# Attention and mixture-of-experts kernel: inputs relaid, projection biases folded into centred weights, norms of tiles 4 to 31 in one chain

## What is computed

```python
x = x + layernorm(attention(layernorm(x)))
x = x + layernorm(ffn(layernorm(x)))
# attention, 16 heads of 8 features
v, q, k = h @ Wv + bv, h @ Wq + bq, h @ Wk + bk
q, k = elu(q) + 1, elu(k) + 1
# causal running sums over the sequence: s += k (outer) v,  z += k
out = (q . s) / (q . z + 1e-6)
return out @ Wo + bo
# ffn: one shared expert, and the best of 16 experts, weighted by sigmoid(logit)
```

## Time and profile before

| | |
|---|---|
| runs | 351.32, 351.48, 351.48 us; median 351.48 |
| profiled execution | 353.47 us, its span 351.6 us |
| TensorE busy | 266.0 us (76%) |
| VectorE busy | 284.8 us (81%) |
| ScalarE busy | 188.8 us (54%) |
| GpSimd busy | 193.1 us (55%) |
| mean granted TensorE clock | 0.912 |
| DMA packets | 20,275, 28.60 MB |

### The profile page before, as it was taken

The page is one execution under the profiler, slowest core; times in us unless marked ns, Lnnn a source line. Parts: engine busy times, 40 slices in busy tenths (PEclk is TensorE's granted clock), DMA queues, the critical chain, the costliest instruction groups (busy, mean ns, idle before and its releaser), DMA issues.

```text
span 351.6 us, 6328 instructions
## 1 busy us (share of the span) xinstructions
PE 266.0 (76%) x1493; PEld 189.3 (54%) x1493; DVE 284.8 (81%) x1147; ACT 188.8 (54%) x572; POOL 193.1 (55%) x221
## 2 busy tenths in 40 slices
PE   0449899999999995838887988730999999999100
PEld 0215565565656552524555755520999988988000
DVE  3599999999999999996998786560279999999940
ACT  1723566565656652447666563301799888885000
POOL 5064677777677773300055556371006888888870
PEclk9998999999999999877999899965699999999855
DMA  4999960000000000000011111126960101110100
GB/s 112 334 427 348 352 203 0 2 3 0 2 0 2 2 0 0 1 3 0 0 63 61 62 62 61 62 76 196 358 207 15 34 30 36 39 36 32 31 2 0
DMA packets 20275, 28.60 MB, mean 81 GB/s; under 512 B 2285, under 2 KB 15476, under 8 KB 19856
## 3 DMA queue, kind: packets, MB, share of 16 engines
q1 hardware_dynamic: 16624, 21.57, 18.2%
q0 software_dynamic: 3040, 6.37, 5.3%
q10 hardware_dynamic: 576, 0.26, 0.3%
HBM read 15.57 MB, written 13.60 MB: 83 GB/s over the span
## 4 chain that ended last, share of the span: by engine, by line
PE 39%; DVE 21%; POOL 17%; issue 12%; DMA 5%; ACT 1%; another core or an unknown queue 1%; SPq 1%; POOLq 0%; ACTq 0%; DVEq 0%
PE banks L1019 13%; POOL out L484 10%; POOL rows L478 5%; PE banks L1042 5%; DMA rows<-in_x 4%; PE banks L1106 3%; PE banks L1140 2%; PE banks L1048 2%; DVE hT L824 2%; POOL sorted_rows L468 2%; PE banks L1007 2%; PE banks L1040 1%; PE banks L1065 1%; PE banks L1063 1%; DVE stats L859 1%
## 5 line engine op out<-in xcount | busy, mean ns | idle before, releaser
L443 POOL TENSOR_TENSOR kv<-qk,vv 128x1024 f32<-128x1024 f32 x32 | 62.5, 1952 | 2.5
L1019 PE MATMUL banks<-kv,upto 128*128 128x512 f32 x128 | 61.3, 602 | 0.8 <-POOL kv L443 0.8
L1140 PE MATMUL banks<-xsT,w_now 128*128 128x128 f32 x376 | 53.8, 288 | 0.4 <-issue 0.4
L484 POOL DMA_INDIRECT out<-rows,token_i x47 | 46.9, 998 | 9.6 <-issue 8.0
L437 POOL TENSOR_TENSOR qk<-ex,rl 128x256 f32<-128x256 f32 x32 | 23.3, 729 | 50.4 <-ACT ex L542 50.4
L1140 PEld LDWEIGHTS banks<-xsT,w_now 128*128 128x128 f32 x376 | 48.1, 200 | 1.2 <-issue 0.5
L468 POOL DMA_INDIRECT sorted_rows<-rows,slot_i x32 | 31.6, 986 | 30.2 <-DVE slot_i L814 22.2
L728 DVE TENSOR_TENSOR prod<-banks,qk 128x1024 f32<-128x1024 f32 x32 | 38.9, 1217 | 2.7 <-PE banks L1019 0.8
L750 DVE TENSOR_REDUCE num<-prod 128x128 f32<-128x1024 f32 x32 | 38.7, 1208 | 0.3 <-DVE den L745 0.3
L958 DVE TENSOR_TENSOR hT_e<-silu_e,banks 128x256 f32<-128x256 f32 x47 | 19.3, 412 | 19.6 <-ACT silu_e L619 14.9
L478 POOL TENSOR_TENSOR rows<-rows,yn 128x128 f32<-128x128 f32 x40 | 19.2, 481 | 28.4 <-DVE yn L950 26.6
(11 more groups left out here) (152 smaller groups left out, 660.6 us busy)
## 6 DMA issues: line engine op xcount, KB each, us to landing
sorted_rows<-rows SPq DMA_DIRECT2D x3, 1950.0 KB, 12.0
rows<-sorted_rows SPq DMA_DIRECT2D x11, 520.0 KB, 6.2
w_exp<-in_gate_up SPq DMA_DIRECT2D x4, 1024.0 KB, 9.2
w_exp_down<-in_down SPq DMA_DIRECT2D x8, 256.0 KB, 8.8
out<-rows,token_i POOLq DMA_INDIRECT x47
rows<-in_x SPq DMA_DIRECT2D x1, 512.0 KB, 8.9
sorted_rows<-rows,slot_i POOLq DMA_INDIRECT x32
rows<-sorted_rows SPq DMA_DIRECT2D x1, 390.0 KB, 5.4
```

The lines of the kernel that those rows point to most:

```text
L443: nc.gpsimd.tensor_tensor(kv[:, u, :].rearrange("p (h m d) -> p h m d", h=NH, m=HD), k, v, ALU.mult).then_inc(s_kv, 1)
L484: nc.gpsimd.indirect_dma_start(out=out_rows, out_offset=bass.IndirectOffsetOnAxis(ap=token_i[:, j - 1:j], axis=0), in_=rows[:, j - 1, 0:D] ...
L1019: ins = nc.tensor.matmul(ps_s[u % 2][:, cols], upto[:], kv[:, u, cols], start=True, stop=True)
L1140: ins = nc.tensor.matmul(ps_gue[u % 2][:, c * P:(c + 1) * P], w_now[:, u % 2, c * P:(c + 1) * P], xsT[:, u % 2, :], start=True, stop=True)
```

## The change

x is given as [128, 32 × 128], so that each partition's tiles follow one another in DRAM. Wq, Wk, Wv and Wo come as one array, so do the four FFN weights, and the expert weights lie partition by partition. The loads are fewer: the four attention weights in one, ahead of x; x in tiles 0 to 3, 4 to 15, 16 to 31; all FFN weights in one; four loads for `w_exp_down` where there were eight.

The q, k and v biases are no longer added by a product per tile. A normed row sums to zero, so taking any constant from all entries of a column of the weights changes nothing. The change makes W' = W − mean of the column + b/128 once, on chip, and norms x to xn + 1 (the shift is raised by 1, one more instruction in `rstd_steps`). A row of ones times W' is b, so (xn + 1) @ W' = xn @ W + b. W' is made by two products into `ps_s[0]`, and VectorE adds them to `w_qkv`. Only bo keeps its three bfloat16 parts, 128 wide.

The norms of tiles 4 to 31 are one chain of `rstd_steps` on VectorE ahead of the attention steps.

```diff
+    if raised:
+        yield series.done(tensor(t, mean2, rs, ALU.mult))
+        series.wait()
+        yield scalar(nm, t, -0.5, 1.0, ALU.mult, ALU.add)
+    else:
+        yield fused(out=nm, in0=mean2, scalar=-0.5, in1=rs, op0=ALU.mult, op1=ALU.mult)
...
+        CHUNKS = [(0, 4), (4, NT)]
+        LOADS = [(0, 4), (4, 16), (16, NT)]
...
+            sp.dma_start(w_qkvo[:], w_att).then_inc(s_w, 16)
+            for c, (t0, t1) in enumerate(LOADS):
                 sp.dma_start(rows[:, t0:t1, 0:D], x_dram[:, t0:t1, :]).then_inc(s_x[c], 16)
...
+            sp.dma_start(w_all[:], w_ffn).then_inc(s_w2, 16)
...
+            nc.gpsimd.memset(bias_rows[:], 0.0).then_inc(s_bias_clear, 1)
             nc.gpsimd.memset(rows[:, NT:ST, :], 0.0).then_inc(s_zero, 1)
...
+            act.dma_start(b_row[:], b_qkv).then_inc(s_b, 16)
+            act.dma_start(bias[:], bo.rearrange("(o d) -> o d", o=1).to_broadcast([P, D])).then_inc(s_bias, 16)
...
-            act.wait_ge(s_bias, 64)
+            act.wait_ge(s_bias, 16)
             act.wait_ge(s_bias_clear, 1)
             bias_row(0)
-            bias_row(1)
...
-                if isinstance(t, int) and t == -3:
-                    bias_row(2)
+                if t in (-2, 0):
+                    bias_row(1 if t else 2)
...
+            nc.vector.memset(mean_row[:], 1.0 / D)
+            nc.vector.memset(neg_mean[:], -1.0 / D).then_inc(s_mean, 1)
...
+            for ins in norm_chunk(0, setup):
                 last = ins
+                next(constants, None)
             last.then_inc(s_norm1, 1)
+            dve.wait_ge(s_fold, 1)
+            nc.vector.tensor_tensor(w_qkv, w_qkv, ps_s[0][:, 0:3 * D], ALU.add).then_inc(s_folded, 1)
+            dve.wait_ge(s_x[1], 16)
+            finish(stats_of(*LOADS[1]))
+            left_of_bias(0)
+            dve.wait_ge(s_x[2], 16)
+            setup.done(finish(stats_of(*LOADS[2])))
+            finish(norm_chunk(1, setup)).then_inc(s_norm1, 1)
             left_of_bias(1)
...
-            run_steps(dve, first_step1, 0, 4, 28, 28, 8, 4)
+            run_steps(dve, step1, 0, 4, 28, 28, 8, 4)
...
                     if isinstance(t, int) and t == -2:
-                        pe.wait_ge(s_const, 2)
-                        pe.wait_ge(s_bias_rows, 3)
-                        pe.wait_ge(s_w, 64)
+                        pe.wait_ge(s_folded, 1)
                     at_least(pe, s_chain, CH * t + Z_READ[odd])
-                    nc.tensor.matmul(ps_qkv[u % 2][:, 0:3 * D], ones_bf[:], bias_rows[:, 0:3 * D],
-                                     start=True, stop=False)
-                    nc.tensor.matmul(ps_qkv[u % 2][:, 0:3 * D], xnT[:, u % 2, :], w_qkv[:],
-                                     start=False, stop=True).then_inc(s_qkv, 1)
+                    nc.tensor.matmul(ps_qkv[u % 2][:, 0:3 * D], xnT[:, u % 2, :], w_qkv,
+                                     start=True, stop=True).then_inc(s_qkv, 1)
...
+            pe.wait_ge(s_mean, 1)
+            pe.wait_ge(s_b, 16)
+            nc.tensor.matmul(ps_s[0][:, 0:3 * D], mean_row[:], b_row[:], start=True, stop=False)
+            pe.wait_ge(s_w, 16)
+            nc.tensor.matmul(ps_s[0][:, 0:3 * D], neg_mean[:], w_qkv, start=False, stop=True).then_inc(s_fold, 1)
             pe.wait_ge(s_const, 1)
```

More of the change, by code:

```diff
@@ L132, in finish, with build @@
     return ins
-def build(nc, x, wq, wk, wv, wo, bq, bk, bv, bo, w_router_t, gate_up, down, w_gate_t, w_up_t, w_down_t, out):
-    B, S, D = x.shape
+def build(nc, x, w_att, b_qkv, bo, w_ffn, gate_up, down, out):
+    B, S, D = out.shape
     NH = 16
     HD = D // NH
-    E = w_router_t.shape[1]
-    F = w_gate_t.shape[1]
+    E = w_ffn.shape[1] % D
+    F = gate_up.shape[1] // (2 * E)
     FC = F // P
@@ L429, in _ @@
             nc.gpsimd.memset(rows[:, 0:NT, TOKEN + 1], 0.0)
-            nc.gpsimd.memset(bias_rows[:], 0.0).then_inc(s_bias_clear, 1)
             def step1(t, u):
@@ L639, in norm_chunk @@
                 return rstd_steps(nc, series, [stats[:, r, n] for n in range(6)], D,
-                                  [scratch1[:, n, r] for n in range(4)], rs1[:, r], nm1[:, r])
+                                  [scratch1[:, n, r] for n in range(4)], rs1[:, r], nm1[:, r], raised=True)
             def constant_steps(series):
@@ L659, in constant_steps @@
                 yield nc.vector.memset(all_ends[:, 0, :], 0.0).then_inc(s_const, 1)
-            dve.wait_ge(s_x[0], 16)
-            setup.done(finish(stats_of(*CHUNKS[0])))
             constants = constant_steps(Series(dve, s_mask_series, 0))
+            for _ in range(3):
+                next(constants)
             def left_of_bias(n):
@@ L671, in left_of_bias @@
                                         ALU.subtract).then_inc(s_bias_left, 1)
-            for n, ins in enumerate(norm_chunk(0, setup)):
+            dve.wait_ge(s_x[0], 16)
+            setup.done(finish(stats_of(*CHUNKS[0])))
+            for ins in norm_chunk(0, setup):
                 last = ins
[L674 to L677, removed]
+                next(constants, None)
             last.then_inc(s_norm1, 1)
-            left_of_bias(1)
[L680 to L688, removed]
-            last_norms = norm_chunk(2, setup)
-            def first_step1(t, u):
-                if isinstance(t, int) and t <= 2:
-                    step1(t, u, norms_of_last_chunk(t), 1)
-                else:
-                    step1(t, u)
-            def norms_of_last_chunk(t):
-                for n in range(NORMS_IN_STEP[t]):
-                    ins = next(last_norms)
-                    if t == 2 and n == NORMS_IN_STEP[t] - 1:
-                        ins.then_inc(s_norm1, 1)
-                    yield ins
+            dve.wait_ge(s_fold, 1)
[6 more added lines that the diff above has]
+            finish(norm_chunk(1, setup)).then_inc(s_norm1, 1)
+            left_of_bias(1)
             def step1(t, u, others=iter(()), between=3):
```

101 lines of the change are left out of this document (50 added, 51 removed).

## The result

The changed kernel takes 347.44 us (median of 4 runs, 347.29 to 347.74) against 351.40 for the kernel before (median of 4). The ratio is 0.9891, with a 95% interval of 0.9874 to 0.9908. It is faster by 3.96 us, where 7.2 were predicted, and lies just above the range of 341.4 to 347.2 us. The profiled execution took 347.56 us, with a span of 345.8.

A forecast was written before the change was run, and what follows sets the result against it. TensorE and VectorE were both taken as full in the steady tiles, TensorE a little more so. Savings of 2.5 + 1.7 + 2.7 + 0.3 = 7.2 us took the median from 351.48 to 344.3 us, range 341.4 to 347.2.

The forecast's parts named there:

- Loads: At the start, x of tiles 0 to 3 lands at 6.1 us, bounds 5.0 and 7.5.
- Norms, fold and the wait that is next: Before tile 0, norms ready at 10.0 us, fold 0.6 us, and ScalarE's first `neg` at 14.4 us against 16.58.
- One chain: Norms of tiles 4 to 31: chain ends at 23.4 us, prod of tile 0 starts 2.5 us earlier, at 24.15.
- Tiles 0 to 3: First three attention steps take 11.5 us instead of 13.26, 1.7 us less, bounds 0.8 and 2.5.
- The steady tiles: Tiles 3 to 27 save 0.22 us a pair, twelve pairs 2.7 us, bounds 2.2 and 3.8.
- End of the stage: End of the attention stage: one L1040 of 0.32 us lies on the chain, so 0.3 us is saved.
- a change of over 1 us from tile 27 to the end: Sign of being wrong: the stretch from tile 27 to the end was to stay as long, within 1 us.
- A: Steady tiles: `att` meets POOL's kv, pays 0.25 us a pair, the steady gain is gone, 347.0 us; chance 0.15.
- C: Start: long runs do little, the last x lands at 18 us, prod of tile 0 at 25.4, 345.6 us; chance 0.07.
- D: Steady tiles: the clock falls to the 1.2 GHz level with less TensorE work, slower at 361.6 us; chance 0.03.
- B: Start and steady tiles: x lands at 5.0 us and the whole 0.32 a pair comes through, 342.1 us; chance 0.13.

The follow-up runs named there:

- e3: The changed kernel with w_att issued behind x of tiles 0 to 3: 343.96 us, ratio 0.9796 to the kernel before.
- e7: The changed kernel with the norms in three chunks as before instead of one chain for tiles 4 to 31: 348.41 us, ratio 0.9952 to the kernel before.
- e6: The kernel before with eleven idle memsets that move its whole VectorE program by 11 places: 353.31 us, ratio 1.0080 to the kernel before.
- e4: The changed kernel with `rden` put ahead of `num` on even tiles: 346.89 us, ratio 0.9907 to the kernel before.
- e2: The kernel before without the bias product L1040 alone, leaving out the q, k and v biases: 351.45 us, ratio 1.0033 to the kernel before.
- e11: The changed kernel run again with no edit: 350.54 us, ratio 0.9891 to the kernel before, which took 354.08 us beside it.
- e8: The changed kernel with x in its first layout, DRAM runs of 512 bytes: 345.16 us, ratio 0.9861 to the kernel before.
- e1: The changed kernel with three idle one-column memsets early in VectorE's program: 345.54 us, ratio 0.9872 to the kernel before.

## Why the prediction was partly wrong

By the profiles the four terms fell 3.4 us short of 7.2: 2.2 in the steady tiles, 0.9 at the start, 0.2 at the end of the stage.

- **Loads: the step that failed.** I put x at 6.1 us, giving w_att 0.75 us by its bytes and taking 0.4 back; it was used at 7.54, just past the bound of 7.5. e3 shows what w_att ahead costs: 3.45 us. It also shows that I gave back too little: with x first, x is used at 4.09, 1.63 us earlier than in the kernel before, where I took 0.4. Which of the fewer loads does this, no run separates. The cost was 2.70 us too small and the gain 1.23 too small; together they make up the 1.44, within 0.03. Bytes over the rate measured later in the stream were the wrong measure: w_att, with nothing ahead of it, takes 2.8 us from issue to landing. The other pieces of x landed in time in the changed kernel: VectorE never waited for them.
- **Norms, fold and the wait that is next.** From x to `neg` I had 8.3 us; it took 7.77. The terms hold: fifteen steps 3.10 against 3.0, the fold 0.55 against 0.6, twelve stats 2.25 against 2.6. So of the 1.44 us by which x was late, 0.9 reached `neg`, at 15.31 instead of 14.4.
- **One chain.** Right in each part: four instructions of POOL in 5.46 us (5.45), three steps that end with them, twelve of 0.22. By the Trainium skill (SBUF — State Buffer, Who interferes with whom) two-input VectorE instructions and POOL's reads lock each other out; the trace agrees for steps one to three (1.54, 0.77 and 1.97 us) and shows 0.19 a step as soon as POOL is out of work. (L101 of the earlier trace rows, on which I leaned, has one input and is no case of that rule.) e7 shows that the chain is a loss for tile 0 and a gain for tile 3. The 0.94 us by which the start fell short are the 0.9 by which `neg` was late.
- **Tiles 0 to 3.** 1.65 against 1.7, but the place was in part luck. The cold tile took 4.78 us, as before (4.76), and not 4.5, and the next two took 6.83. The whole gain is the step from tile 1 to 2, 5.29 to 3.56, where a norm step of the kernel before was held under kv. How much of it is seen depends on the kernel before: e6 takes 15.80 there with the same work.
- **The steady tiles: the other step that failed, twice.** First the size: 0.16 us a pair came through where I took 0.22, below my lower bound of 0.18. Only the step from an even to an odd tile shrank, from 3.30 to 3.14; the other stayed at 3.93. I take it for VectorE's: e4, which only moves an instruction of VectorE, shortens it to 3.84. By then VectorE had nothing left to give: outside tile 22 it is as full as TensorE. Its idle 0.18 a pair, my lower bound, held the pause at tile 9 too, which no saving on TensorE frees. Second the lock at tile 22, which takes back 1.64. Twelve pairs of 0.16 and the pause at tile 9 are 2.2 us; less 1.64 it is the 0.54 measured.
- **End of the stage.** 0.07 against 0.3: the L1040 on the chain there was worth nothing, since VectorE is busy 31.99 of the 33.80 us from 123.2 to 157; e2, which lacks it too, takes 24.16 us from tile 27 to 31 against 24.14. I had named a change of over 1 us from tile 27 to the end as a sign of being wrong. The profiles have 224.7 us before, 222.6 after and 227.1 in e11, so the same code differs by more than that, and the sign says nothing.
- **Rivals.** A named the right collision, VectorE against kv, but the wrong instruction and number: `att` kept its 0.28 and 0.52 us, and `rden`, with 0.20 us of room before (it began at 82.89, kv at 83.10) and 0.05 after, met kv once instead of twelve times. That A's 347.0 us lies nearest to the 347.44 measured is luck. C was right that the long runs do nothing (e8), but its condition did not come: the last stats began at 14.54 without a wait, so x had landed by then and not at 18, and VectorE's stats, not x, set the chain's start. D did not come: the clock stays at 1.00 in the steady stretch. B failed with x.

In short, the mechanisms were right; the landing of x was mis-sized by 1.44 us, the pair by 0.06, and one lock was not seen. With x at 7.54, a pair of 7.07 and 0.07 at the end the same sum gives 5.5 us, and less the lock 3.8.

## What to carry to other kernels

Put the transfer that the first instruction needs ahead of all others on its queue; 256 KB ahead of it delayed its use by 3.45 us here and the first tile by 2.34, more than the 1.9 us that folding the biases gained in the steady tiles. When a change brings POOL and VectorE closer together, measure the room between each short VectorE instruction and POOL's next long one, and leave more than the 0.35 us by which VectorE can be late for no reason in the code. A product removed from one of two full engines was worth no more here than the other's idle time, 0.16 of 0.32 us a pair.

## What the hardware did that was not expected

- VectorE starts one instruction 0.35 us late at a fixed place of its program, at record 191 in the kernel before and in e2, and 319 in the changed one, e3, e6, e8 and e11 (counted from 0), each time a `num` with a wait just ahead of it. It moves with padding (e1, e6). The instruction queue has two packets from 100 to 108 us in the changed kernel, at 105.56 and 106.93, 0.57 us ahead of the late start and 0.80 behind it. The kernel before has one from 60 to 68 us, at 64.37, 0.68 behind its late start at 63.69. The queue in both stretches, changed and before (packets, MB, share):

```profile
q14 instruction: 2, 0.02, 0.7%
```

```profile
q14 instruction: 1, 0.01, 0.4%
```

  So the pause is not the wait for a packet that lands just ahead of it, since the kernel before has none there. A packet follows 0.66 to 0.80 us behind the late `num` in each of seven profiles (before, changed, e2, e3, e6, e8, e11). That both come from one place in the program is likely; what VectorE waits for stays open.
- A 16-column add, `rden`, takes 1.67 to 1.93 us instead of 0.17 when it begins under POOL's kv, though it has one input. The same holds for `upto` at 1.88 us: 3.38 us beside a memset of POOL that begins at 1.84 and takes 3.34, which reads nothing. The Trainium skill (SBUF — State Buffer, Who interferes with whom) says that `tensor_scalar` can run in a mode that takes both ports, and that whichever of VectorE and GpSimd issues first then keeps the shared pair for its whole instruction while the other is blocked. Both rows agree: VectorE's instruction began second and ended with POOL's.
- Longer runs in DRAM did not speed x up, with its pieces in SBUF still 512 bytes: x was used at 7.54 us with them and at 6.66 without (e8).
